# A third buffer of h, re-ordered parts, and two multiplications and subtractions moved from VectorE to GpSimd

## The reference

```
h = layernorm(x) * (1 + ca) + sa
val, gate = split(h @ W_in)                      # 512 channels each
val = silu(conv3(val))                           # over time, one filter for each channel
B, C = val @ W_B, val @ W_C                      # 16 states each
Delta = softplus((val @ W_delta + base) @ W_tau)
A_bar = exp(Delta * A); B_bar = expm1(Delta*A) / (Delta*A + 1e-6) * Delta * B
h_t = A_bar * h_(t-1) + B_bar * val;  y_t = sum over 16 states of h_t * C_t
x = x + ga * (y * silu(gate) @ W_out + h)
h = layernorm(x) * (1 + cb) + sb
x = x + gb * (2 of 8 experts by a sigmoid router + one shared expert; each W1, gelu, W2, 256 hidden)
```

## Time and profile before

| | us |
|---|---|
| median of 3 runs (lowest, highest) | 5493.48 (5478.98, 5497.39) |
| the profiled execution's own time | 5478.18 |
| its span | 5476.4 |
| first scan starts | 272.4 |
| busy: PE / DVE | 4017.3 / 4403.8 |
| busy: ACT / POOL | 4051.8 / 3658.4 |
| TensorE clock granted, mean | 0.842 |

### The profile page before, as it was taken

The page is one execution under the profiler, slowest core; times in us unless marked ns, Lnnn a source line. Parts: engine busy times, 40 slices in busy tenths (PEclk is TensorE's granted clock), DMA queues, the critical chain, the costliest instruction groups (busy, mean ns, idle before and its releaser), DMA issues.

```text
span 5476.4 us, 36465 instructions
## 1 busy us (share of the span) xinstructions
PE 4017.3 (73%) x9708; PEld 1675.1 (31%) x9708; DVE 4403.8 (80%) x3862; ACT 4051.8 (74%) x4199; POOL 3658.4 (67%) x2132
## 2 busy tenths in 40 slices
PE   7531415787787878787888888787877875959889
PEld 3210102233333333333333333333333332323343
DVE  1388799989898898989888889989898989889210
ACT  2586777888888887888888887888888877878111
POOL 0299876677777776777777777676777777777211
PEclk8765657898888898898889898898889896979889
DMA  4487867677676767677677767676676666677322
GB/s 137 152 256 226 250 154 208 174 212 197 194 206 198 209 181 229 169 218 192 193 210 199 204 190 214 175 219 191 185 214 199 194 181 188 181 201 187 122 92 73
DMA packets 338776, 1037.14 MB, mean 189 GB/s; under 512 B 40197, under 2 KB 43141, under 8 KB 331270
## 3 DMA queue, kind: packets, MB, share of 16 engines
q1 hardware_dynamic: 274058, 799.91, 44.3%
q0 software_dynamic: 64512, 234.91, 22.0%
HBM read 673.29 MB, written 126.51 MB: 146 GB/s over the span
## 4 chain that ended last, share of the span: by engine, by line
DMA 23%; issue 19%; PE 17%; DVE 16%; ACT 12%; POOL 11%; POOLq 0%; SPq 0%; DVEq 0%; ACTq 0%
DMA ysum<-hs 22%; POOL hs L1282 6%; PE ps L1023 6%; DVE ps L1077 3%; DVE ps L1084 3%; PE ps L1039 3%; PE ps L993 3%; DVE ps L1071 3%; ACT inv L675 2%; POOL hid L1310 2%; DVE xa L1144 2%; POOL inv L1298 1%; ACT th L682 1%; DVE ps L1091 1%; PE ps L984 1%
## 5 line engine op out<-in xcount | busy, mean ns | idle before, releaser
L1298 POOL TENSOR_TENSOR inv<-inv,th 128x1024 f32<-128x1024 f32 x512 | 1331.2, 2600 | 275.3 <-ACT th L682 275.2
L1282 POOL TENSOR_TENSOR hs<-hs,Cb 128x1024 f32<-128x1024 f32 x512 | 1249.7, 2441 | 262.9 <-DVE hs L1104 227.6
L1039 PE MATMUL ps<-w2r,hid 128*128 128x512 f32 x2304 | 1142.9, 651 | 19.8 <-DVE x L1130 19.7
L1023 PE MATMUL ps<-hf,w1r 128*128 128x512 f32 x2304 | 1131.0, 646 | 2.9 <-DMA w1r<-in_W 2.3
L1050 PE MATMUL ps<-Brow,pick 48*128 48x512 bf16 x1024 | 362.3, 439 | 997.3 <-DVE hs L1104 996.7
L670 ACT ACTIVATE inv<-nrd,kappa 128x1024 f32<-128x1024 f32 x512 | 557.4, 1140 | 383.0 <-DVE ps L1084 379.0
L682 ACT ACTIVATE th<-delta,halfA 128x1024 f32<-128x1024 f32 x512 | 582.7, 1138 | 279.3 <-POOL inv L1298 279.3
L1104 DVE TENSOR_TENSOR_SCAN hs<-abar,ps 128x1024 f32<-128x1024 f32 x256 | 583.5, 2279 | 234.2 <-DMA ysum<-hs 231.1
L1291 POOL DMA_DIRECT2D ysum<-hs x448 | 391.9, 875 | 509.9 <-issue 399.8
L1104 DVE TENSOR_TENSOR_SCAN hs<-abar,carry,ps 128x1024 f32<-128x1024 f32 x256 | 598.7, 2338 | 158.5 <-DMA ysum<-hs 158.3
L1071 DVE TENSOR_TENSOR ps<-ps,us 128x1024 f32<-128x1024 f32 x512 | 627.5, 1226 | 79.0 <-PE ps L1050 41.7
(11 more groups left out here) (150 smaller groups left out, 4870.2 us busy)
## 6 DMA issues: line engine op xcount, KB each, us to landing
Cb<-c_rows SPq DMA_DIRECT2D x512, 512.0 KB, 4.9
ysum<-hs POOLq DMA_DIRECT2D x448, 512.0 KB, 6.6
w2r<-w_scaled SPq DMA_DIRECT2D x144, 512.0 KB, 8.0
w1r<-in_W SPq DMA_DIRECT2D x144, 512.0 KB, 4.3
gbc<-expert_gates SPq DMA_DIRECT2D x128, 256.0 KB, 3.7
aw<-in_W_val SPq DMA_DIRECT2D x64, 256.0 KB, 7.9
xa<-in_x SPq DMA_DIRECT2D x16, 1024.0 KB, 8.5
h_residual<-hT SPq DMA_DIRECT2D x16, 1024.0 KB, 11.1
```

Of the source, the lines that this page charges most:

```text
L1023: mm = t.matmul(o, w1r[:, n % 2, k, h * P:(h + 1) * P], hf[:, k, :], start=(k == 0), stop=(k == G - 1))
L1039: mm = t.matmul(o, hid[:, e % HB, h, tt * P:(tt + 1) * P], w2r[:, e % 3, h, :], start=(grp < 2 and e % 3 == 0 and h == 0), stop=(e % 3 == ...
L1282: gp_.tensor_tensor(hs[:, c % 2, :], hs[:, c % 2, :], Cb[:, c % 2, :], ALU.mult).then_inc(hC_done, 1)
L1298: gp_.tensor_tensor(inv[:, c % 6, :], inv[:, c % 6, :], th[:, c % 2, :], ALU.mult).then_inc(thinv_done, 1)
```

## The change

The edits, in the order of the diff:

- `hs` gets a third buffer, so the scan of c waits for the addition of state c-3; `us` gets a second one, with its load in slots 8 and 24 in place of 14 and 30. The room comes from `hid`, which loses two of six buffers; `hidden(p)` puts two of the experts' hidden blocks into `xn` in their place.
- GpSimd's slot is re-ordered: `times_C(c - 1)`, then the parts of the slot, then `weight(c + 2)`, and last the addition to y (`add_to_y(c - 1)`) with its waits.
- y times gate is issued by GpSimd in slots 1 and 17, after `times_C` and ahead of the weight; the softplus's subtraction by GpSimd in slots 16 and 20 (`log1p`), and VectorE's second half of the softplus moves from slot 19 to 20.
- On ScalarE the square root of the second normalisation moves to the start of w = 2, the sigmoid to "squared" of w = 3, the normalisation of `xa` to "squared" of w = 6, and evictions of t, t2 and w1 to other places.
- On TensorE the jobs of slots 14 to 17 and 27 to 29 are spread differently, and the times for which banks are planned are changed with them.
- On VectorE the statistics of x1 are taken tile by tile in slots 6, 7 and 8, the two `rstd_of` stand late in slots 9 and 25, the copy of B and C in slot 13.

```
@@ -109,14 +109,14 @@
...
         nrd = sb("nrd", [P, 2, TB])
-        us = sb("us", [P, TB])
+        us = sb("us", [P, 2, TB])
...
         abar = sb("abar", [P, 4, TB])
-        hs = sb("hs", [P, 2, TB])
+        hs = sb("hs", [P, 3, TB])
...
         hf = sb("hf", [P, G, T])
-        hid = sb("hid", [P, HB, HT, T])
+        hid = sb("hid", [P, HB - 2, HT, T])
...
+
+        def hidden(p):
+            i = p % HB
+            return xn[:, 2 * (i - 3):2 * (i - 3) + 2, :] if i in (3, 4) else hid[:, i if i < 3 else 3]
...
@@ -511,12 +516,12 @@
...
-            if r in (14, 30) and 0 <= c // N + 1 < NU:
+            if r in (8, 24) and 0 <= c // N + 1 < NU:
                 u = c // N + 1
                 if u % G == 0:
                     sp.wait_ge(st_u, 32 * (u // G + 1))
-                ge(sp, uB_done, N * u)
-                sp.dma_start(us[:], u_d[u // G, u % G]).then_inc(us_ld, 16)
+                ge(sp, uB_done, N * (u - 1))
+                sp.dma_start(us[:, u % 2, :], u_d[u // G, u % G]).then_inc(us_ld[u % 2], 16)
...
-            if r in (16, 19) and has(qa):
-                gp = r // 19
+            if r in (16, 20) and has(qa):
+                gp = r // 20
                 sp.wait_ge(delta_done, 2 * qa + gp + 1)
                 store_half(delta_d, qa, 2 * gp, 2 * gp + 2, pre[:, 2 * gp:2 * gp + 2, :]).then_inc(st_delta, 16)
...
@@ -795,7 +800,7 @@
                 if w == 2:
                     if place == "squared":
                         take_gate(qa, (2, 3))
-                    if place == "half logs" and has(qf):
+                    if place == "start" and has(qf):
                         act.wait_ge(f_stat, (TPB + 1) * (qf + 1))
                         s.activation(rstdF[:, :, 0], momF[:, :, 1], ACT.Sqrt, bias=consts[:, 0:1]).then_inc(f_sqrt, 1)
                     if place == "logs":
@@ -805,18 +810,19 @@
                     if place == 1:
                         take_p(qa, (2, 3))
                     if place == 2:
+                        take_t2(qf, (0, 1))
+                    if place == 3:
+                        take_t2(qf, (2, 3))
                         softplus_exp(qa, 0)
-                    if place == 3:
-                        take_t2(qf, (0, 1))
                 if w == 3:
                     if place == "start":
-                        take_t2(qf, (2, 3))
                         softplus_exp(qa, 1)
                     if place == "logs":
                         softplus_ln(qa, 0)
-                    if place == 0 and has(qf):
+                    if place == "squared" and has(qf):
                         act.wait_ge(mm_log, qf + 1)
-                        s.activation(ps[:, bank_of["log", qf, 0], 0:TPB * E], ps[:, bank_of["log", qf, 0], 0:TPB * E], ACT.Sigmoid).then_inc(ev_log, 1)
+                        score = ps[:, bank_of["log", qf, 0], 0:TPB * E]
+                        s.activation(score, score, ACT.Sigmoid).then_inc(ev_log, 1)
                     if place == 1:
                         take_w1(qf, 0)
                     if place == 2:
@@ -829,11 +835,11 @@
                         softplus_ln(qa, 1)
                     if place == 0:
                         take_w1(qf, 3)
+                    if place == 2:
+                        take_w1(qf, 4)
                     if place == 3:
-                        take_w1(qf, 4)
+                        take_w1(qf, 5)
                 if w == 5:
-                    if place == "start":
-                        take_w1(qf, 5)
                     if place == "logs":
                         gelu(qf, 1)
                 if w == 6:
@@ -846,18 +852,17 @@
                         take_w1(qf, 7)
                     if place == 0:
                         take_w1(qf, 8)
-                    if place == 1 and has(qn):
+                    if place == "squared" and has(qn):
                         act.wait_ge(a_rstd, 2 * qn + 2)
                         for tt in range(TPB):
                             ins = s.activation(xa[:, tt, :], xa[:, tt, :], ACT.Identity, bias=rstdA[:, tt, 1:2], scale=rstdA[:, tt, 0:1])
                         ins.then_inc(a_xn, 1)
+                    if place == 3:
+                        take_t(qn, (0, 1))
                 if w == 7:
                     if place == "start":
+                        take_t(qn, (2, 3))
                         gelu(qf, 2)
-                    if place == "squared":
-                        take_t(qn, (0, 1))
-                    if place == "half logs":
-                        take_t(qn, (2, 3))
...
-                13: [("log", qf, 0), ("w1", qf, 0)], 14: [("w1", qf, 1), ("w1", qf, 2)],
-                15: [("gT", qf, 0), ("w1", qf, 3), ("w1", qf, 4)], 16: [("w1", qf, 5), ("w1", qf, 6)],
-                17: [("w1", qf, 7)], 18: [("w1", qf, 8), ("w1", qf, 9)], 19: [("w1", qf, 10)],
+                13: [("log", qf, 0), ("w1", qf, 0)], 14: [("w1", qf, 1)],
+                15: [("w1", qf, 2), ("gT", qf, 0), ("w1", qf, 3)], 16: [("w1", qf, 4), ("w1", qf, 5)],
+                17: [("w1", qf, 6), ("w1", qf, 7)], 18: [("w1", qf, 8), ("w1", qf, 9)], 19: [("w1", qf, 10)],
                 20: [("w1", qf, 11), ("w2", qf, 0)], 21: [("w2", qf, 1)], 22: [("w2", qf, 2)], 23: [("w2", qf, 3)],
                 24: [("w1", qf, 12), ("w1", qf, 13)], 25: [("w1", qf, 14), ("w1", qf, 15)], 26: [("w1", qf, 16), ("w1", qf, 17)],
-                27: [("w2", qf, 4)], 28: [("w2", qf, 5), ("t", qn, 0), ("t", qn, 1)], 29: [("w2", qf, 6), ("t", qn, 2), ("t", qn, 3)],
+                27: [("t", qn, 0), ("t", qn, 1), ("w2", qf, 4)], 28: [("w2", qf, 5), ("t", qn, 2), ("t", qn, 3)], 29: [("w2", qf, 6)],
                 30: [("w2", qf, 7)], 31: [("val", qn, 0), ("val", qn, 1)],
...
-            held = {"t": (29, 29, 30, 30), "val": (1.5, 2.5, 3.5, 3.9), "gate": (8.3, 8.4, 9.5, 9.6), "p": (10.9, 11, 11.4, 11.5),
-                    "bc": (14,), "t2": (12, 12.1, 12.6, 12.7), "log": (14.95,), "gT": (15.9,),
-                    "w1": (14.4, 14.5, 15.4, 15.5, 16.5, 16.6, 18, 18.1, 19.3, 19.4, 20.9, 21, 25.3, 25.4, 25.8, 25.9,
-                           26.5, 26.6)}[kind]
+            held = {"t": (28.7, 28.7, 29.5, 29.5), "val": (1.5, 2.5, 3.5, 3.9), "gate": (8.3, 8.4, 9.5, 9.6), "p": (10.9, 11, 11.4, 11.5),
+                    "bc": (14.6,), "t2": (12, 12.1, 12.6, 12.7), "log": (14.95,), "gT": (15.9,),
+                    "w1": (15.4, 15.5, 15.9, 16.3, 17, 17.2, 19.4, 19.5, 20.6, 20.7, 21, 21.1, 25.1, 25.2, 25.8, 25.9,
+                           27.4, 27.5)}[kind]
...
-                    if c >= 2:
-                        if (c - 2) % N < 2:
-                            dve.wait_ge(y_begun, unit(c - 2) + 1)
+                    if c >= 3:
+                        if (c - 3) % N < 2:
+                            dve.wait_ge(y_begun, unit(c - 3) + 1)
                         else:
-                            dve.wait_ge(y_summed, 16 * sums(c - 2))
+                            dve.wait_ge(y_summed, 16 * sums(c - 3))
                     first = (u // G) % (L // TB) == 0
-                    v.tensor_tensor_scan(hs[:, c % 2, :], abar[:, c % 4, :], X(c),
+                    v.tensor_tensor_scan(hs[:, c % 3, :], abar[:, c % 4, :], X(c),
                                          0.0 if first else carry[:, u % G, c % N:c % N + 1], ALU.mult, ALU.add).then_inc(scan_done, 1)
...
-            def gate_y(u):
-                if 0 <= u < NU:
-                    dve.wait_ge(y_summed, 16 * (N - 2) * (u + 1))
-                    dve.wait_ge(gate_ld, 16 * (u + 1))
-                    v.tensor_tensor(gy[:], ysum[:], gy[:], ALU.mult).then_inc(y_gated, 1)
...
             def softplus(q, gp):
                 if has(q):
                     part = slice(2 * gp, 2 * gp + 2)
-                    dve.wait_ge(a_ln, 2 * q + gp + 1)
-                    v.tensor_tensor(lnw[:, part, :], lnw[:, part, :], tt1[:, part, :], ALU.subtract).then_inc(a_log1p, 1)
...
-                if r == 10 and has(qf):
+                if r == 8 and has(qf):
+                    dve.wait_ge(ev_out, TPB * (qf + 1))
+                    tile_stats(x1, statsF, f_stat, (3,))
+                    mean_and_variance(statsF, momF, f_stat, qf * (TPB + 1))
+                if r in (1, 2, 3):
+                    convolve(qa, r - 1)
+
+            def late():
+                if r == 25 and has(qn):
+                    dve.wait_ge(a_sqrt, qn + 1)
+                    rstd_of(rstdA, momA, a_rstd, qn)
+                if r == 9 and has(qf):
                     dve.wait_ge(f_sqrt, qf + 1)
                     rstd_of(rstdF, momF, f_rstd, qf)
-                if r == 26 and has(qn):
-                    dve.wait_ge(a_sqrt, qn + 1)
-                    rstd_of(rstdA, momA, a_rstd, qn)
-                if r in (1, 2, 3):
-                    convolve(qa, r - 1)
-
-            def late():
-                if r in (1, 17):
-                    gate_y(c // N - 1)
                 if r in (2, 3, 4, 5):
```

(71 more changed lines are left out.)

18 lines of the change are left out of this document (10 added, 8 removed).

## The result

The changed kernel takes 5169.55 us (median of 4 runs, 5168.17 to 5178.88), the kernel before 5487.01 beside it. The ratio is 0.9424, with a 95% interval of 0.9402 to 0.9446. The prediction was 5200 us.

The account below looks back on a forecast made before the run. No engine was full: three hand one wait round, VectorE nearest the bound. GpSimd's 275 us plus 11 of loss made a 286 us window; 245 us from twelve windows plus 45 elsewhere gave 5188, predicted as 5200 us, range 5020 to 5410.

Parts of the forecast that it names:

- The third buffer: VectorE's scans waiting for the accumulating DMA into `ysum`: seven waits go, 0 to 22.8 us saved in a window.
- GpSimd's slots: GpSimd's work and DMA landings in the new order: 259 us, 271 with long landings, mean 275 with carry copies.
- long landings: GpSimd's waits for DMA landings that outlast their slot: 4 to 24.8 us a window, taken as 12.
- the first rival: GpSimd has room, landings shrink and VectorE's work is the bound: windows of 268 us, about 4970 us; chance 0.14.
- The waits for tanh: GpSimd's waits for ScalarE's tanh: parts done ahead of the weight hide most of 19.9 us, about 4 stay.
- The normalisation of xa: ScalarE's normalisation, moved ahead of the logarithms, waits for VectorE's late result: 0 to 6.1 us a window, taken as 2.
- The other parts: Moved evictions, square root, sigmoid, TensorE's jobs and loads of `us`: covered by idle time, so they change no sum.
- The moves: y times gate and softplus's subtraction, VectorE to GpSimd: 12.6 us off VectorE, 10.2 onto GpSimd in a window.
- The other windows: Gains outside the twelve full windows: 5, 13, 15 and 12 us in windows 0, 1, 14 and 15; start and tail nothing.
- The sum: GpSimd 275, VectorE 263, ScalarE 253 us, plus 11 for joining them: a window of 286 us, 20.4 less.

Follow-up runs that it names:

- e1: The kernel before with the third buffer of h alone (and the hidden blocks in `xn` that make room for it); 5404.2 us, ratio 0.9846.
- e3: The changed kernel with two buffers of h in place of three; 5576.5 us, ratio 1.0160 to the kernel before.
- e9: The changed kernel with GpSimd's old slot order and only 128 of 1024 columns of C's row loaded from state 2 on; 5259.4 us, ratio 0.9591.
- e10: The changed kernel with the normalisation of xa back at its old place on ScalarE; 5099.2 us, ratio 0.9301 to the kernel before.
- e5: The kernel before with the third buffer of h and GpSimd's new slot order, nothing else; 5252.3 us, ratio 0.9583.
- e2: The changed kernel with y times gate and the softplus's subtraction back on VectorE; 5223.0 us, ratio 0.9517 to the kernel before.
- run 64: Not a follow-up run: "run" is a verb here, the same eight matmuls are executed 64 times in the changed kernel.
- after: As a kernel's name: the changed kernel with all edits, against the kernel before; 5169.55 us, ratio 0.9424.

## Why the prediction was right

- **The third buffer.** Right for the wait: that of the scans went from 22.8 to 1.6 us in the window. The time is another matter. Alone the buffer took 380 us off that wait over the run and only 85 us off the time (e1). What the prediction had not said is that buffer and order need each other (e1, e3).
- **GpSimd's slots.** I counted 259 us and 12 of long landings, 271. In window 7 GpSimd is busy 225.6 us and waits 18.0 + 5.1 us for landings, 249 together, so my slots were 22 us too long. The waits weren't the error: my 12 stood beside about 12 more inside the slots (ten times 0.6, twice 3.2). The error is that I added up the durations of instructions that overlap. The issue of the DMA runs beside the product that follows, so in the order of time below a slot without a part takes 5.2 us, from issue to issue, where I had 6.0 of work:

```profile
2410.17 0.86 POOL L1294 DMA_DIRECT2D ysum<-hs  x1
2410.78 2.64 POOL L1282 TENSOR_TENSOR hs<-hs,Cb 128x1024 f32<-128x1024 f32 x1
2413.10 2.62 POOL L1307 TENSOR_TENSOR inv<-inv,th 128x1024 f32<-128x1024 f32 x1
2415.41 1.14 POOL L1294 DMA_DIRECT2D ysum<-hs  x1
```

The landing of 6.6 us that I used was too long by 1.4; e9 shows that it was the row of C beside it, which stood only in the first rival.
- **The waits for tanh.** Wrong: of 19.9 us I let 4 stay, 22.0 stayed. Over the whole run they grew from 275.2 to 349.8 us, and e10 brings them back to 274.9, so in this kernel the growth hangs on the moved normalisation on ScalarE. It isn't the only cause, for e5 has the old place and 319.2 us. That GpSimd does its parts earlier and then waits for the same tanh is how I read it; no run shows it by itself. The 18 us that this term was too small and the 22 that the slots were too large cancel in the window. That part of the agreement is luck.
- **The normalisation of xa.** The place was right and the size not: 2 us of a window, 4.8 measured (e10), within its bound of 6.1. The wait for `rstdA` that I had named is 40.6 us over 14 windows, 2.9 each. Beside it stands one that I hadn't, that of TensorE, whose jobs I had counted as covered: 30 us to spare in a window is no cover in a slot whose job waits for a bank.
- **The other parts.** I let the moved evictions, TensorE's jobs and the loads of u change no sum. Against e5 they are worth about 100 us by the estimate above, and the normalisation takes 70 of them back. That the two largely cancel is luck too.
- **The moves.** y times gate gave 47 to 71 us of the 82 that L1124 took on VectorE. The subtraction, priced at 7.6 us a window, gave nothing that can be told: the instruction that needs its result is the next of VectorE in the same slot, a wait that the prediction didn't name. L1146 takes 1.2 us with nothing in its way and 3.4 beside one product of GpSimd. The rule in the Trainium skill (SBUF — State Buffer, Who interferes with whom), that the two exclude each other for a whole instruction, agrees with that. It doesn't give the two cases of 8.9 us, in which GpSimd runs three products one behind the other. The rule in the Trainium skill (GPSIMD Engine Reference, Engine selection), that GpSimd takes about twice as long, agrees in its factor (GpSimd 2.36 us, VectorE 1.2 at its best) and not in what follows from it for y times gate.
- **The other windows.** Window 0 gained 22 us where I had 5 (310 against 288); my own figures, 310 less 278 less 10.2, leave 22 and not 5. Window 1 gained 9 where I had 13, 14 and 15 together 28 where I had 27. The tail and the start became 6 and 7 us longer, where I had nothing.
- **The sum.** 20.4 us a window predicted, 22.0 measured. The first rival needed VectorE as the only bound: its work is 269 us in window 7 and 259 in window 8, and 12 and 24 us of idle are left there. Its faster landings came, its windows of 268 us didn't. ScalarE and TensorE late in single slots are a part of that: without the lateness of slot 27 a window takes 279.6 us (e10).

What stays open: how much of the 29 us between e5 and e2 belongs to the second buffer of u, which wasn't run alone, and how the loss of 70 us divides.

## What to carry to other kernels

A buffer and the order of the engine that empties it are one edit: count the path from the buffer's use to its release under the new order before adding or saving a buffer. Work moved to another engine takes time off the first only if nobody there waits for the result in the same slot. Durations of one engine's instructions can overlap: take the length of a slot from the order of time and not from the sum of the groups. When an engine shows spare time over a window, check the slots in which its job waits for a bank before calling it a cover.

## What was not expected of the hardware

After the 6.7 us without work TensorE ran eight matmuls in 6.13 us that take 3.70 us at 2810.1, and the table of windows shows the mean granted clock in the two stretches, 0.59 and 1.00 of 2.4 GHz:

```profile
2801.80:2807.80 6.00, 6.00 (x9) 2.60 (x10) 3.18 (x3) 6.00 (x7) 5.92 (x5) 0.59 0.46 87
2810.10:2813.70 3.60, 3.60 (x10) 1.69 (x10) 3.52 (x3) 2.99 (x4) 3.52 (x4) 1.00 1.01 322
```

So this late job on TensorE is also a slow one, and its 2.4 us more are a part of VectorE's wait of 4.9 us. It isn't alone: the same eight matmuls run 64 times in after, 11 times behind a wait of 4.7 to 7.1 us, and these take 5.1 to 6.7 us; the 53 others have no wait ahead and take 3.6 to 3.7. And two transfers of 512 KB sent off together cost the accumulating one 1.4 us on top of 5.2.
